# Layer norms beside narrow attention: who makes the normalised rows

## The reference

```
def _ln(x):
    mu = mean(x, axis=-1);  var = var(x, axis=-1)
    return (x - mu) * rsqrt(var + EPS)
h = _ln(x) * (1 + scale) + shift          # per batch and channel
x = attention(h, h) + x
x = attention(_ln(x) modulated, context) + x
x = mlp(_ln(x) modulated) + x
```

## Time and profile before

| | |
|---|---|
| median of 3 runs | 4248.3 us (4246.96 to 4249.77) |
| profiled execution, its own time | 4261.02 us |
| span in the profile | 4258.8 us |
| mean granted TensorE clock | 0.958 of full |
| busy: PE / DVE / ACT / POOL | 3869.4 / 2935.5 / 2059.4 / 1429.4 us |

### The profile page before, as it was taken

One profiled execution on the slowest core, in us unless ns is written; L12 is line 12 of the kernel. 1 busy time (PEld: TensorE's weight loads), 2 busy tenths in 40 slices (PEclk: granted clock), 3 DMA queues, 4 the chain that ended last, 5 costly groups with the idle time before them and its releaser, 6 DMA issues. The chain is left out here.

```text
span 4258.8 us, 53349 instructions
## 1 busy us (share of the span) xinstructions
PE 3869.4 (91%) x19532; PEld 2328.2 (55%) x19532; DVE 2935.5 (69%) x4277; ACT 2059.4 (48%) x3724; POOL 1429.4 (34%) x728
## 2 busy tenths in 40 slices
PE   7999988899997889998999968987999999998989
PEld 5333347533334665555555546666555555546777
DVE  5888855788866567786777835545778777774465
ACT  2666655366664534444444436643444444445641
POOL 1100122110013146665666544320444444451120
PEclk8999989899998989999999989998999999999999
DMA  4233240322234423323333233232232233215320
GB/s 131 37 64 42 47 81 16 60 43 46 36 54 75 80 62 68 70 50 67 66 66 63 44 84 78 67 82 62 69 70 61 58 70 70 62 36 127 78 56 21
DMA packets 151829, 268.09 MB, mean 63 GB/s; under 512 B 33946, under 2 KB 67668, under 8 KB 150544
## 3 DMA queue, kind: packets, MB, share of 16 engines
q1 hardware_dynamic: 151568, 264.67, 29.7%
HBM read 103.96 MB, written 29.64 MB: 31 GB/s over the span
## 5 line engine op out<-in xcount | busy, mean ns | idle before, releaser
L1020 PE MATMUL PS<-t 128*128 128x512 f32 (+4 forms) x7896 | 1963.4, 380 | 129.1 <-DVE t L1677 16.5
L1478 ACT ACTIVATE t<-PS 128x512 f32<-128x512 f32 (+2 forms) x1600 | 1166.8, 750 | 1003.6 <-PE PS L1020 995.3
L1020 PEld LDWEIGHTS PS<-t 128*128 128x128 f32 (+2 forms) x7896 | 1236.3, 185 | 654.7 <-issue 236.7
L1199 PE MATMUL PS<-t 128*32 128x512 f32 (+2 forms) x4352 | 811.6, 612 | 0.0
L1762 DVE TENSOR_REDUCE t<-PS 128x1 fp32r<-128x1024 f32 x512 | 618.0, 1218 | 231.7 <-PE PS L1092 230.8
L1768 DVE TENSOR_REDUCE t<-PS 128x1 f32<-128x512 f32 x1024 | 644.9, 681 | 60.0 <-PE PS L1096 56.1
L2057 POOL TENSOR_TENSOR t<-t 128x1024 f32<-128x1024 f32 x256 | 621.4, 2427 | 119.5 <-ACT t L1478 94.5
L1092 PE MATMUL PS<-t 128*128 128x512 f32 x1024 | 337.5, 412 | 68.2 <-DVE t L1762 39.4
L1096 PE MATMUL PS<-t 96*128 96x512 bf16 x1024 | 358.7, 393 | 35.7 <-DVE t L1768 20.8
L2053 POOL TENSOR_TENSOR t<-t 128x1024 f32<-128x1024 f32 x64 | 153.9, 2404 | 692.0 <-PE PS L1209 531.9
L1199 PEld LDWEIGHTS PS<-t 128*32 128x32 f32 (+2 forms) x4352 | 170.7, 122 | 326.8 <-issue 324.0
(11 more groups left out here) (133 smaller groups left out, 3520.6 us busy)
## 6 DMA issues: line engine op xcount, KB each, us to landing
t<-t SPq DMA_DIRECT2D x640, 128.0 KB, 2.5
t<-scr_n SPq DMA_DIRECT2D x288, 128.0 KB, 6.6
t<-t SPq DMA_DIRECT2D x128, 256.0 KB, 3.8
scr_n<-t SPq DMA_DIRECT2D x72, 256.0 KB, 2.6
t<-t SPq DMA_DIRECT2D x256, 64.0 KB, 2.0
t<-in_L_Wg SPq DMA_DIRECT2D x16, 768.0 KB, 4.5
t<-in_L_W SPq DMA_DIRECT2D x36, 256.0 KB, 3.5
t<-in_L_Wo SPq DMA_DIRECT2D x64, 128.0 KB, 2.4
```

What stands on the lines that cost most here:

```text
L1020: ins = e.matmul(out, l, r, start=i == 0, stop=i == len(terms) - 1, tile_position=tp)
L1199: ins = e.matmul(banks[S.ot][wd * j:wd * j + wd, :], u.v[j][kt], P[0:S.pr, j, :], start=kt == 0, stop=kt == S.nkt - 1, tile_position=(0, w ...
L1478: e.activation(dst, src, ACT.Exp, scale=S.L.scale).then_inc(*expd.inc((S.i, i)))
```

## The change

The 64 `ln_norm` instructions of the eight parts of `on_pool` (four in each narrow layer, eight tiles each) are issued by GpSimd and no longer by VectorE, with the same operands, the same waits and the same place in the plan. The other 128 stay on VectorE, as do all statistics, the epsilon and the reciprocal. The signal `ln_normed` becomes two, one for each engine, and `ln_turn` and `ln_bias` wait for that of the part's engine. Since GpSimd now reads the statistics, `ln_stats` of a part waits until the norms of the part before it, if made by GpSimd, are done.

```
-    ln_normed = signal("ln_normed")
+    ln_normed = [signal("ln_normed_v"), signal("ln_normed_p")]
...
-                w.wait_ge(ln_normed, (p.i, 2 * q + 1))          # tensor, ln_turn
+                w.wait_ge(ln_normed[on_pool(p)], (p.i, 2 * q + 1))
...
             elif what == "ln_stats":
                 p, t = a
                 T = 8 * p.b + t
+                if p.i and on_pool(line[p.i - 1]):
+                    w.wait_ge(ln_normed[1], (p.i - 1, 7))
...
-            elif what == "ln_norm":
+            elif what == "ln_norm" and not on_pool(a[0]):       # vector
...
+            elif what == "ln_norm" and on_pool(a[0]):           # gpsimd
+                p, t = a
+                if t >= 4 or p.i:
+                    k, nth = where[("ln", p.i, t // 2 - 2) if t >= 4 else ("ln", p.i - 1, 2 + t // 2)]
+                    w.wait_ge(bank_full[k], nth)
+                w.wait_ge(ln_recip, p.i)
+                e.tensor_scalar(XN[:, t % 4, :], X[:, 8 * p.b + t, :], ln_mv[:, t, 0:1], ln_sd[:, t:t + 1],
+                                ALU.subtract, ALU.mult).then_inc(*ln_normed[on_pool(p)].inc((p.i, t)))
```

More of the change, by code:

```diff
@@ L1654, in vector_program @@
                 e.tensor_scalar(XN[:, t % 4, :], X[:, 8 * p.b + t, :], ln_mv[:, t, 0:1], ln_sd[:, t:t + 1],
-                                ALU.subtract, ALU.mult).then_inc(*ln_normed.inc((p.i, t)))
+                                ALU.subtract, ALU.mult).then_inc(*ln_normed[on_pool(p)].inc((p.i, t)))
             elif what == "ln_split" and not on_pool(a[0]):
@@ L1978, in gpsimd_program @@
                 w.wait_ge(row_in, p.i)
-                w.wait_ge(ln_normed, (p.i, 7))
+                w.wait_ge(ln_normed[on_pool(p)], (p.i, 7))
                 x = X[:, 8 * p.b:8 * p.b + 8, :]
@@ L1982, in gpsimd_program @@
                                 ).then_inc(*biased.inc(p.i))
+            elif what == "ln_norm" and on_pool(a[0]):
[5 more added lines that the diff above has]
+                e.tensor_scalar(XN[:, t % 4, :], X[:, 8 * p.b + t, :], ln_mv[:, t, 0:1], ln_sd[:, t:t + 1],
+                                ALU.subtract, ALU.mult).then_inc(*ln_normed[on_pool(p)].inc((p.i, t)))
             elif what == "ln_split" and on_pool(a[0]):
```

## The result

The change made the kernel slower. Seven runs of it have a median of 4266.0 us (4259.2 to 4269.9), seven of the kernel before 4248.5 us (4245.2 to 4258.8); the ratio is 1.0035, with a 95% interval of 1.0024 to 1.0047, which is 10 to 20 us. I had forecast 4244 and a range of 4233 to 4257. The changed kernel's profiled execution took 4266.04 us, with a span of 4264.3 us; the one of before was 12.7 us over its median, so the two spans differ by only 5.5 us, and I compare stretches rather than spans.

The account below looks back on a forecast made before the run. TensorE was taken to bound plain self-attention units, VectorE only some with norms. Self-attention -5.4 us plus cross-attention 2 x (0.3 + 0.5) made -3.8 us, so 4244 us; range 4233 to 4257.

Parts of the forecast that it names:

- The price of one norm on GpSimd: One moved norm instruction on GpSimd, no row showing it there: taken as 0.45 us, between 0.31 and 1.26.
- part (1,1): Cross-attention: first two norms 0.3 us later per layer, later pairs hidden between GpSimd's splits; ends +0 and +4.9.
- part (2,0): Cross-attention with weight splits in GpSimd's queue: late norms and split against relieved VectorE, +0.5 us per layer; ends -1.5, +6.
- Rival B: Cross-attention: dear norms in GpSimd's queue between splits, decided from 0.6 us each; at 0.9, +9.4 us, 4258; chance 0.15.
- The sum's sign: Whole kernel: self-attention's gain of 5.4 us in two layers outweighs cross-attention's loss, -3.8 us in all.
- part (0,1): Self-attention: three norms leave unit 0, bound by VectorE, gaining 1.0 us per layer; ends 0 and 1.3.
- part (1,0): Self-attention: unit from 1121.94 us gains 1.4, the next 0.3, so 1.7 us per layer; ends 0.9 and 2.8.
- The excess of 0.8 us in unit 10: Self-attention unit from 1121.94 us: 1.4 us over plain units, transposes 0.60, so at least 0.8 is VectorE's.
- Rival A: VectorE bounds all self-attention where norms lie, cross-attention even: -14 us, 4234; chance 0.23.
- The stalls of VectorE behind GpSimd: Norms held back by the shared port, such as one of 1.32 us at 1139.08 us: the blocking goes with the norm.
- The order of events: Cross-attention: TensorE's first wait grows to 5.1 us; norms between weight split and HF split delay it, and ScalarE waits longer.
- Rival C: Nothing comes of it: TensorE fills what VectorE sheds, or VectorE and GpSimd share a port in turns; 4248, chance 0.20.

Follow-up runs that it names:

- half: The changed kernel, but GpSimd normalises only 128 of 256 columns beside cross-attention; median 4265.1 us, ratio 1.0014 to the kernel before.
- self_only: Against the kernel before, GpSimd makes only the 32 norms beside narrow self-attention; median 4254.2 us, ratio 0.9999.
- cross_v: The kernel before, with the splits beside cross-attention moved from GpSimd to VectorE as well; median 4259.4 us, ratio 1.0006.

## Why the prediction was wrong

- **The price of one norm on GpSimd** is the step that failed. I said 0.45 us, with ends at 0.31 and 1.26; it is 1.22. All else of the size follows. The upper ends of my own working, +4.9 for part (1,1) and +6 for part (2,0), met +4.1, and +5.1 and +6.5 in the two layers. Rival B had the mechanism, GpSimd's queue between two splits, and its deciding point of 0.6 us holds as far as half (0.8 us, slower by 6 us) can tell. But I priced B at 0.9 and gave it 0.15, and cut the range at 4257, below B's own 4258, with an end in hand that led to +16. Bounds by two other forms said nothing of a third, and the value in the middle was taken by likeness. The Trainium skill's sentence on one-input work (GPSIMD Engine Reference, Engine selection), which I cited beside it, is not far off for the rounding copy of 128x512 (0.61 us on GpSimd, 0.42 on VectorE) and does not hold for this form (1.22 against 0.41 us, the medians); the measurement decides.
- **The sum's sign.** Self-attention was to give 5.4 us and gave 1.1: part (0,1) 0.0 instead of 1.0, part (1,0) 0.6 instead of 1.7 per layer. Unit 0 looked bound by VectorE in the earlier trace rows, busy 22.89 of 25.09 us; in the changed kernel it is as long to 0.01 us. Idle time of TensorE in a unit was an upper end, and I used it as the value. The excess of 0.8 us in unit 10, which I called VectorE's, gave 0.15 at most; the statistics, the root and its wait on ScalarE stayed where they were. Rival A is refuted by the same numbers.
- **The stalls of VectorE behind GpSimd**, that of the earlier trace rows among them, went with the norms, as said. The two units where they stood in self-attention gained no more than the 0.6 us above.
- **The order of events** in cross-attention came as predicted: the first wait of TensorE grew (4.84 to 6.67 us, forecast 5.1 at the wrong price), in part (2,0) the split of the second pair stood behind a weight split and the two norms of the third, and ScalarE waited 3.67 us for it in layer 0. The plain units didn't change (24.66, 24.82, 25.40 and 25.44 us before, 24.67, 24.83, 25.40 and 25.44 after).
- **Rival C** had self-attention right: what VectorE no longer does gave TensorE nothing that can be told (self_only 0.9999). Its shared port is not what the changed kernel lost by, since VectorE's other instructions took no longer; cross_v shows that it can cost 4 us at one blow.

## What to carry to other kernels

An instruction that moves to another engine has the price of its own form there; when the trace has no row of that form, a bound by likeness is none, and the far end belongs in the range. A helper engine with a low busy share can still be the chain of a stage: count what stands in its queue between two steps that others wait for, and compare that with the gap it had. And an engine that is level with the bound can cost time when work is added and give none back when work is taken.

## What the runs showed of the hardware

- GpSimd's two-operation form with one tensor in costs 0.37 us and 3.33 ns a column, measured from 128 to 1024 columns; with one operation at 256 columns 0.85 to 0.92 us; the subtraction of two tensors 0.72 us and the copy 0.40 us.
- A rounding copy on VectorE, 0.42 us alone, took 4.62 us beside a bias addition of 4.50 us on GpSimd: it ended 0.28 us after it. This is what the Trainium skill states of the two engines' shared ports (SBUF — State Buffer, Who interferes with whom), with a stall of 4.2 us where that of the earlier trace rows was 0.9.
- The same stretch of work differs by some us within an execution and between executions: cross-attention of the kernel before took 115.6 us in layer 0 and 120.1 in layer 1, at a mean granted clock of 0.85 both times. Unit 2 of its self-attention, without any norm, took 31.67 us in layer 0 at full clock and 33.44 in layer 1 at 0.95. The plain units, at full clock throughout, repeat to 0.03 us in all kernels (the first of them 24.66 to 24.69), and so does the time from reciprocal to last split in part (1,1), 12.71 to 12.73 us in the kernels that leave that part as before; that is where small effects can be read.
